# Two routers take statistics ahead of a normalisation, and the scan's copy unit makes no diagonal blocks

## The reference, cut to what matters

```python
x = x + 0.5 * L0_ffn(layernorm(x))      # mixture of experts: "m1"
x = x + L0_attn(layernorm(x))           # causal attention, 16 heads: "a1", "a2"
x = x + 0.5 * L0_ffn(layernorm(x))      # mixture of experts again: "m2"
x = x + 0.5 * L1_ffn(layernorm(x))      # channel mix: "c1"
x = x + L1_attn(layernorm(x))           # selective scan: "s1", "s2", "s3"
x = x + 0.5 * L1_ffn(layernorm(x))      # channel mix, in "s3"
```

```python
state = exp(delta * A) * state + delta * Bm * uc       # over 1024 time steps
y = sum over the states of state * Cm
```

## Time and profile before

| | |
|---|---|
| median of 3 runs | 4616.25 us (4610.25 to 4618.79) |
| profiled execution | 4618.48 us, its span 4616.8 us |
| busy share of the span | PE 87%, DVE 66%, POOL 51%, ACT 50% |
| router of m1 | from the start to about 78.5 us |
| router of m2 | about 1769 to 1901 us |
| scan s2 | about 2975 to 4254 us |

### The profile page before, as it was taken

One profiled execution on the slowest core, in us unless ns is written; L12 is line 12 of the kernel. 1 busy time (PEld: TensorE's weight loads), 2 busy tenths in 40 slices (PEclk: granted clock), 3 DMA queues, 4 the chain that ended last, 5 costly groups with the idle time before them and its releaser, 6 DMA issues. The chain is left out here.

```text
span 4616.8 us, 118840 instructions
## 1 busy us (share of the span) xinstructions
PE 4004.6 (87%) x49612; PEld 2548.5 (55%) x49612; DVE 3047.8 (66%) x5270; ACT 2330.9 (50%) x3872; POOL 2372.3 (51%) x1536
## 2 busy tenths in 40 slices
PE   4499798899999997459979799699999999997799
PEld 3366454233333334336647444387787778776577
DVE  6411154888888875631137477599899899997575
ACT  2122143577777772012226378667777776774233
POOL 1144434222222224124523265399999999998454
PEclk7699899899999998679989999899999999998899
DMA  7323366655555636233332466633333443342662
GB/s 213 110 47 50 74 216 218 95 94 94 94 94 94 94 62 219 90 101 51 52 75 74 142 241 245 216 90 97 99 95 94 102 100 94 96 102 81 248 226 82
DMA packets 339596, 549.37 MB, mean 119 GB/s; under 512 B 55488, under 2 KB 239200, under 8 KB 339040
## 3 DMA queue, kind: packets, MB, share of 16 engines
q1 hardware_dynamic: 285552, 467.46, 38.6%
q0 software_dynamic: 24576, 34.10, 4.6%
q10 hardware_dynamic: 28912, 40.02, 2.4%
HBM read 335.69 MB, written 212.32 MB: 119 GB/s over the span
## 5 line engine op out<-in xcount | busy, mean ns | idle before, releaser
L2532 POOL TENSOR_TENSOR s_hc<-s_hs,s_ct 128x1024 f32<-128x1024 f32 x512 | 1214.4, 2387 | 66.8 <-DVE s_hs L2511 51.5
L2511 DVE TENSOR_TENSOR_SCAN s_hs<-s_dA,s_psB 128x1024 f32<-128x1024 f32 x512 | 1169.0, 2286 | 100.2 <-POOL s_hc L2532 29.0
L2435 PE MATMUL s_psB<-s_diag,s_duT 128*32 128x128 f32 x32768 | 961.1, 274 | 80.0 <-DVE s_hs L2511 44.0
L2435 PEld LDWEIGHTS s_psB<-s_diag,s_duT 128*32 128x32 f32 x32768 | 909.0, 111 | 184.0 <-issue 102.4
L1382 DVE CUSTOM_DVE_ANT_0 a_masked<-a_psM,k_later 128x1024 f32<-128x1024 f32 (+7 forms) x1024 | 724.6, 750 | 146.7 <-PE a_psM L1440 144.2
L1364 ACT ACTIVATE a_wt<-a_psE 128x512 f32<-128x512 f32 (+1 forms) x1216 | 625.6, 578 | 268.3 <-PE a_psE L1466 258.9
L2376 ACT ACTIVATE s_dA<-s_dlt,s_aneg 128x1024 f32<-128x1024 f32 x512 | 587.6, 1148 | 341.2 <-DVE s_hs L2511 335.9
L1343 POOL TENSOR_SCALAR_AFFINE_SELECT a_wt<-a_wt 128x512 f32<-128x512 f32 x256 | 163.2, 637 | 692.9 <-ACT a_wt L1364 692.8
L2356 ACT ACTIVATE s_diag<-s_ident,s_bt 128x128 f32<-128x128 f32 x956 | 317.5, 388 | 13.4 <-ACT s_ys L2365 13.4
L1440 PE MATMUL a_psM<-a_kst,a_qst 96*128 96x512 bf16 (+3 forms) x1152 | 306.0, 330 | 14.4 <-DVE a_mx L1382 10.6
L1466 PE MATMUL a_psE<-a_qst,a_kst 99*128 99x512 bf16 (+3 forms) x1152 | 308.8, 329 | 7.6 <-ACT a_wt L1364 6.5
(11 more groups left out here) (366 smaller groups left out, 6236.0 us busy)
## 6 DMA issues: line engine op xcount, KB each, us to landing
s_dlt<-dd SPq DMA_DIRECT2D x128, 512.0 KB
a_qst<-qs SPq DMA_DIRECT2D x144, 128.0 KB
a_kst<-ks SPq DMA_DIRECT2D x144, 128.0 KB
yd<-s_ys ACTq DMA_DIRECT2D x33, 512.0 KB
vs<-a_va ACTq DMA_DIRECT2D x32, 512.0 KB, 3.6
zsd<-s_zs SPq DMA_DIRECT2D x32, 512.0 KB, 2.7
ucd<-s_uc SPq DMA_DIRECT2D x8, 2048.0 KB, 9.3
dd<-s_dl SPq DMA_DIRECT2D x32, 512.0 KB, 4.1
```

The costliest lines, as they stand in the source:

```text
L2435: ins = pe.matmul(psB[s][DG * m:DG * (m + 1), c * P:(c + 1) * P], duT[j % 2][:, c, DG * r:DG * (r + 1)], diag[:, place(NB * g + m, u), c, ...
L2511: dve.tensor_tensor_scan(hs[k % 2][:, :], dA[k % 2][:, :], psB[s][:, :], 0.0, ALU.mult, ALU.add).then_inc(scanned, 1)
L2532: pool.tensor_tensor(hc[NB * (g % 2) + r][:, :], hs[k % 2][:, :], ct[:, g, :], ALU.mult).then_inc(weighed, 1)
```

## The change

In both routers DVE's loop for b becomes: the statistics of b + 2 (in m2 with the sums ahead of them), then the norm of b + 1. Before, the norm of b + 1 came first. The logits of b - 1, which stood behind the norm, stand behind the statistics in m1, and in m2 between the third and the fourth of the sums. In `rstds` POOL waits for its own rstd of b - 1 before it writes `veps` again. In the scan `due` skips unit 69: the blocks that would be due from 69 on are due a unit later.

```diff
 def rstds(b):
     pool.wait_ge(stats_ready, b + 1)
+    if b:
+        pool.wait_ge(rstd_ready, b)
...
-def summed(b):
-    dve.wait_ge(xb_ready, b + 1)
-    for k in range(4):
+def summed(b, parts):
+    if 0 in parts:
+        dve.wait_ge(xb_ready, b + 1)
+    for k in parts:
...
-stat(0)
-gathered(0)
-stat(1)
-normed(0)
-gathered(1)
+for b in range(2):
+    if front:
+        summed(b, range(4))
+    stat(b)
+    if b:
+        normed(0)
+    gathered(b)
 for b in range(B):
-    if b + 1 < B:
-        normed(b + 1)
-    if b:
-        logits(b - 1)
+    if front and b + 2 < B:
+        summed(b + 2, range(3))
+        if b:
+            logits(b - 1)
+        summed(b + 2, (3,))
     if b + 2 < B:
         stat(b + 2)
         gathered(b + 2)
+    if b and not (front and b + 2 < B):
+        logits(b - 1)
+    if b + 1 < B:
+        normed(b + 1)
 logits(B - 1)
...
+SUMS_OUT = 5
 def due(n, c):
...
-    return 60 + ((n - 2 * NB) * NC + c) // 5
+    k = 60 + ((n - 2 * NB) * NC + c) // 5
+    return k + 1 if k >= UPB + SUMS_OUT else k
```

More of the change, by code:

```diff
@@ L378, in stat @@
                     if front:
-                        summed(b)
                         dve.wait_ge(y_ready, 4 * (b + 1))
@@ L2387, in step @@
                                              psB[slot[t]][:, :]).then_inc(turn_copied, 1)
-                            if q == 5:
+                            if q == SUMS_OUT:
                                 out(b if j else b - 1, (j - 1) % IT_)
```

## The result

The changed kernel took 4633.06 us (median of 6 runs, 4628.99 to 4633.82), the kernel before 4618.56 us beside it. The ratio is 1.0035, 95% interval 1.0024 to 1.0046. The forecast was 4607.0 with a range of 4599 to 4628. Its sign and its range were both wrong.

A forecast was written before the change was run, and what follows sets the result against it. Stages stand one behind the other, with DVE and the round trip to POOL bounding m1. The terms -12.3 (m1) + 9 (m2) - 6.5 (scan) sum to -9.8 us, 4606.5 on the runs' median, rounded to 4607; range 4599 to 4628.

The forecast's parts named there:

- m1: First router: statistics ahead of the norm hide the 2.11 us rstd wait; norms 6.17 apart; -12.3 us, bounds -10.5 and -14.
- the waits for the turned logits of 5 and of 6: End of m1, no statistics left as cover: `logits(5)` waits 2.1 (PE at its faster pace) to 3.2 us.
- The power: POOL's operation for rstd, beside m1's norms: doesn't hold DVE, becomes 0.1 us longer itself; counted as nothing.
- the rival that it holds VectorE: Routers: power blocks DVE for all its 1.67 us in m1's norms, m2's norms 1 to 4 cut too; 4640; chance 0.03.
- Scan: Exp behind the copy of `psY` starts 1.57 us earlier, shortening the next scan's wait; -6.5 us, bounds -8.5 and -3.
- four copies: Scan: of five copies with waits of 1.7 to 1.8 us, four gain 1.5 each, 6.0 in all.
- m2: Second router: new order makes a closed chain through PE, 17.5 us a sequence against 17.13; +9 us, bounds +3 and +14.
- the stall of 4.2 and the rstd wait of 2.1: m2: both delays at DVE's norm, from POOL's bias addition and rstd, are gone; the wait for PE replaces them.
- The rival: m2: bias addition cuts into norms 1 to 4, 17 to 21 us in all, about 4626; more or fewer cuts 0.27.
- what was added for the power and the operation ahead of it: m2: 0.1 us for the power and as much for the operation ahead move the addition's start from 2.05 to 2.15 to 2.3.
- the 0.8 for a PE that was idle longer: m2, in the rival of the cut norm: perhaps 0.8 us per cut, on top of 4.3 in the closed chain.
- the closed chain: m2: norm b, transposes, turn, heads of b + 2, sums, statistics, norm b + 1; 16.7 to 18.3 us, taken as 17.5.

The follow-up runs named there:

- e4: Kernel before with only the first router's (m1) new VectorE order, plus POOL's added wait in `rstds`: 4605.66 us, ratio 0.9974.
- e3: Kernel before with only the scan's `due` change, plus POOL's added wait in `rstds`: 4607.99 us, ratio 0.9983.
- e7: e5 with PE computing the heads of b + 2 ahead of the turn of b: 4568.34 us, ratio 0.9893 to the kernel before.
- e2: Kernel before with only m2's new VectorE order, plus POOL's added wait in `rstds`: 4652.61 us, ratio 1.0075.
- e5: Changed kernel with POOL's bias addition to b + 2 waiting for norm b - 1: 4607.52 us, ratio 0.9982 to the kernel before.
- e6: e1 with POOL's bias addition to b + 2 waiting for norm b: 4570.50 us, ratio 0.9892 to the kernel before.
- e1: Changed kernel with m2's VectorE order put back as before: 4595.67 us, ratio 0.9959 to the kernel before.
- e9: Changed kernel with only PE's order changed, heads of b + 2 ahead of the turn of b; addition not held: 4569.01 us, ratio 0.9908.
- e10: e6 with PE computing the heads of b + 2 ahead of the turn of b: 4565.34 us, ratio 0.9896 to the kernel before.

## Why the prediction was wrong, step by step

**m1, right.** Forecast -12.3 in bounds of -10.5 and -14; the next stage starts 12.7 us sooner, and e4 as a whole gave -12.0. The norms start 6.06 apart (6.17 forecast), the waits for the turned logits of 5 and of 6 are 1.90 and 1.91, a little under the 2.1 to 3.2 forecast. The power, which I put at nothing, takes 1.74 to 1.95 beside the norm and leaves it at 2.65 to 2.67: the rival that it holds VectorE is refuted in all six norms.

**Scan, right in size, and only in part in its working.** Forecast -6.5 in bounds of -3 and -8.5; e3 gave -7.8, and the stage is 7.6 us shorter in the mean of the traces. The forecast counted 1.5 us for each of four copies. Of these the one at 3486.33 has a wait of 1.13 for PE in place of ACT's in the changed kernel, and in e3 two of the four have one (1.47 and 1.46). Single traces differ by more than such a wait: e3's stage is 1264.2 us long, e7's 1256.9. What moves PE's waits there stays open.

**m2, wrong, and it decides the sign.** Forecast +9; e2 gave +34.6, and the trace +36.4. Two steps make the difference.

The first is "the stall of 4.2 and the rstd wait of 2.1 are gone". The rstd wait is gone, the stall is not: it moved from the norm's first instruction to its eighth. The rival had this to the point. It saw the two instructions within 0.1 us of one another, and the addition then started 2.11 after the aggregation's end (1792.85 to 1794.96), at the lower end of the 2.05 to 2.3 that it names. But what was added for the power and the operation ahead of it, 0.1 and more, came out differently: the power's record is 0.28 longer, and the addition starts 0.3 before that record ends. So the rival was the case and not the forecast, and I had given it 0.27. It was priced low as well: 17 to 21, where a cut sequence is 23.92 and an uncut one 18.34, four times 5.6 = 22.3 us. The 4.3 of the cut norm were right; the 0.8 for a PE that was idle longer is 1.3, since the 24 matmuls of the heads take 6.74 to 6.79 behind a cut norm and 5.50 behind the whole one (in e5 5.34 to 6.35). Where the outcome hangs on 0.1 us, four cuts of 4.5 us stand against a gain of nothing; that would have asked for even chances and, by the upper bounds of the parts (-10.5 + 14 - 3 + 22.3 = +22.8), for a range to nearly 4640.

The second is the size of the closed chain. The forecast took 17.5 a sequence, between 16.7 (PE fast) and 18.3 (PE slow). Measured without any cut: 18.3 in e5, so its slower end. PE idles 4.5 us a sequence, and 12 of its transposes then take 2.72 to 2.79, as at the granted clock of 0.50 in the earlier trace rows; in e5 it is 0.50 too, in the windows from 1816 to 1819. That is 0.8 a sequence, 4 to 5 us in all. e5's router is 13.9 longer than before, against a bound of +14.

Together: 13.9 for the new order without a cut and 22.6 for the cut are, before rounding, the 36.4 us of the trace.

The comparison that the forecast never made is with the old order, uncut. It counted the end of the stall as a gain of the new order, though the stall belongs to neither order: e6 shows that one wait on POOL takes 26.0 us off the old one (25.5 against e1), and e5 22.6 off the new. So the 13.9 of e5 are two things, a closed chain of +39.9 (e5 less e6) and an undone stall of -26.0.

The Trainium skill (SBUF — State Buffer, "Who interferes with whom") says that the shared port pair goes to whichever starts first for its whole instruction, and that on VectorE's side it takes a mode with two ports or two inputs from SBUF. With the bias addition that agrees throughout: one `tensor_scalar` lasts 4.72 behind it in place of 0.4, and 0.54 more than alone when it comes in pieces, while the sums (one input in PSUM) and the statistics lose nothing. With the power of 128x8 it does not agree as "fully blocks": in m2 the norm takes 2.65 and the power 1.94 instead of 1.67, side by side.

## What to carry to other kernels

Before an order is changed around a stall, ask whose the stall is. Here it was a collision of two engines, and one wait that puts the long GpSimd instruction behind VectorE's row took 26.0 us off the router with DVE's old order and 22.6 with its new one, 0.5 to 0.6% of the whole time. With PE's heads first it wasn't measured by itself, as most cuts were gone there without it. When work is moved ahead on one engine, follow the chain once round the loop: an order that takes the other engine's output earlier needs that engine's order changed with it. And a collision that the numbers put within 0.1 us is to be priced as one that may well happen.

## What the runs showed that was not expected

- GpSimd gets in between two instructions of a dense row on VectorE. The addition that starts 0.04 us ahead of the eighth `tensor_scalar` makes it last 4.72 instead of 0.4.
- POOL's power takes 1.94 beside `tensor_scalar` in m2, 1.74 to 1.95 in m1, and 1.67 alone; the next POOL instruction starts up to 0.3 us before that record ends.
- A collision can vanish because something else gets faster: in e9 a load that lands 0.2 to 2.6 us later than POOL could use it moves the addition out of the norm's way, in three norms of four.
- Three different orders (e6, e7, e10) come to 11.0 to 11.2 us a sequence, but for the first three of e10 with 10.8. In e7 PE waits 0.98 for ACT's copies and is busy for the rest; whether the transfers, busy at the same time (DMA share 1.07 in its windows, 363 GB/s), would be the next bound was not tried.
